# Two edits to a fused transformer-and-MoE kernel: where the last jobs' normalisation stands, and which instruction re-orders the tokens

## The chip, the cores and the metric

The kernel runs on one core of one Trainium2 chip. The time is the device time of one execution in microseconds; for the kernel before it is the median of three runs. One core has TensorE (PE; its weight loads are PEld), VectorE (DVE), ScalarE (ACT), GpSimd (POOL) and SyncE (SP), which here only issues DMAs. Each engine works through its own list in order and waits on semaphores for the others.

## What is computed

```python
x = x + 0.5 * ffn(layernorm(x))        # 16 sequences of 256 tokens, 128 features, fp32
x = x + dilated_attention(layernorm(x))
x = x + 0.5 * ffn(layernorm(x))

def ffn(x):      # 16 heads of 8, causal; 8 experts, top 2, F = 512
    h = layernorm(x + attention(x) @ w_o, g1, b1)
    w = top-2 softmax gates of h @ wg, renormalised
    y = gelu(h @ w1[e] + bb1[e]) @ w2[e] + bb2[e]      # for the two experts of a token
    return layernorm(h + sum_e w[e] * y[e], g2, b2)
```

The dilated attention takes every fourth token (DILATION_RATE 4) of a sequence, 64 at a time, and attends inside such a slice. So each sequence has two token orders in the kernel: the natural one, which the causal attention needs, and one sorted by offset, in which the rows are held for everything else.

## The kernel before

The rows are cut into 8 chunks of two sequences (512 tokens, 4 tiles of 128). Each of the two FFN layers passes over all chunks, which makes 16 jobs: jobs 0 to 7 are the first FFN, jobs 8 to 15 the second. Two jobs make a set; a set's tokens are sorted by expert, scattered to DRAM, read back in tiles of 128 rows of one expert, put through that expert's two layers, stored, and gathered again by token. The set of jobs 14 and 15 is the last, and its gathers end the program.

For one job m the pieces are: `norm`, `norm_apply` (first layer norm, VectorE), `turn` (TensorE transposes the four tiles into a bank of `ps_ring`, ScalarE copies the bank to `xn_t`), `project` and `values` (the projections, which read `xn_t`), the attention proper (`scores`, `exps`, `weigh`, `rows`), `merge` (TensorE transposes the attention's result, ScalarE copies it to `attn_feat`), `attn_out` and the middle norm, the router, the set's expert tiles (`turn_tiles`, `first`, `second`), and at the end `gather` (GpSimd), `combine`, `end_norm`, `end_norm_apply`, `end_add` (VectorE, with a power taken on GpSimd for each norm) and `store` (SyncE).

The order of pieces in each engine's list is fixed before the kernel is built: `make_orders` gives every piece a place (a half step plus a number from the table PLACES, by kind, stretch of the program and position in the set) and sorts by it. Nothing is moved at run time.

The two places that matter here:

- **The re-ordering copies.** In `turn` (TensorE L621, ScalarE L850) the transposes write tokens in the order sorted by offset, next to each other, and ScalarE's copy puts them into natural order while it writes `xn_t`. In `merge` (TensorE L729, ScalarE L884) the transposes write natural order and ScalarE's copy writes `attn_feat` sorted by offset. The copies `project` (L860) and `long_turn` (L916) are of the same size, 128x512, without re-ordering. There are 16 jobs, so 16 copies and 64 transposes at each of the two places.
- **The end of the last two jobs.** Job 14's rows are gathered with 8 indirect DMAs (L1406, two for each tile), combined (L1235, L1241), their statistics taken (L970, L974), the variance plus epsilon written (L977), and GpSimd raises it to the power -0.5 (L1344). VectorE meanwhile centres the rows and multiplies by g2 / 2 (`scale_centred`, L1201) and then adds them, scaled by the power, to the rows held in `xs` (`add_scaled`, L1212). Job 15 does the same tile by tile (`combine_last`, L1176 to L1194), since its gathers signal tile by tile, then `finish_last` (L1224) adds. SyncE stores a job's rows in four DMAs (L591); job 14's wait for `add_scaled`, job 15's in two pairs for `finish_last`. At the end all engines' queues close with a DRAIN and a barrier (L326).

Two semaphore and buffer slots are used for these norms: END for both jobs, that is, `var_eps[:, END]` and `rstd[:, END]`.

## Time and profile before

| what | value |
|---|---|
| median of three runs | 1115.26 us (1113.8 to 1119.22) |
| the profiled execution's own time | 1125.35 us |
| its span | 1123.6 us |
| TensorE busy | 969.8 us (86%) |
| TensorE weight loads busy | 788.8 us (70%) |
| VectorE busy | 687.5 us (61%) |
| ScalarE busy | 664.3 us (59%) |
| GpSimd busy | 569.8 us (51%) |
| DMA | 182.51 MB, mean 162 GB/s |

The profiled execution is a single one and is not among the three runs; its time lies 1.75 us above its span. Busy times are sums over the whole span, which has a start in which the first chunk goes through alone, a long body in which two or three jobs and the expert tiles overlap, and an end in which only tiles, then only gathers are left. A busy share says little about what an engine is worth in one of these, so the rows below are cut by stretch.

### The profile page before, as it was taken

To read this page: it belongs to the slowest core of one execution; us is meant where nothing else is said; L and a number is where in the kernel's file an instruction comes from. 1 tells how busy PE (TensorE), PEld (TensorE's weight loads), DVE (VectorE), ACT (ScalarE), POOL (GpSimd) and SP (SyncE) were. 2 spreads that over 40 slices of the span, in tenths; PEclk is the share of its full clock that TensorE was granted. 3 is DMA by queue.
4 is the path that set the end of the run, shared out by engine and by line. 5 is a ranking of instruction groups with operands and counts; after the bars stand their busy time and mean duration, and the time that the engine had idled before them with its cause. 6 is when DMAs were issued, how large, how long until landed. Compare 5 with 4: busy or idle time off the path is not lost.

```text
span 1123.6 us, 29725 instructions
## 1 busy us (share of the span) xinstructions
PE 969.8 (86%) x10913; PEld 788.8 (70%) x10913; DVE 687.5 (61%) x2458; ACT 664.3 (59%) x1494; POOL 569.8 (51%) x693
## 2 busy tenths in 40 slices
PE   3898987999899999999899998999899988947860
PEld 2666655887677877778777877788777876846860
DVE  6657784665457865798557955697567734620234
ACT  1333533777567766777657785678667767633530
POOL 2234365334565556655564555654674466550434
PEclk9978978999889999999989998999999999986985
DMA  2496043466665556556664546566575655786741
GB/s 70 103 204 165 15 118 104 128 180 170 164 173 159 156 173 132 192 170 190 161 186 146 162 166 145 166 183 195 151 197 163 191 160 161 258 257 228 265 146 47
DMA packets 120199, 182.51 MB, mean 162 GB/s; under 512 B 13144, under 2 KB 83192, under 8 KB 120056
## 3 DMA queue, kind: packets, MB, share of 16 engines
q1 hardware_dynamic: 111864, 163.83, 50.5%
q0 software_dynamic: 8192, 16.79, 5.1%
q8 instruction: 88, 1.44, 0.5%
q14 instruction: 55, 0.45, 0.2%
HBM read 145.10 MB, written 40.19 MB: 165 GB/s over the span
## 4 chain that ended last, share of the span: by engine, by line
PE 63%; DVE 13%; ACT 7%; another core or an unknown queue 6%; issue 5%; POOL 4%; DMA 1%; SPq 0%; POOLq 0%; DVEq 0%; ACTq 0%
PE ps_ring L796 12%; PE ps_ring L787 11%; PE ps_quad L657 6%; PE ps_quad L690 6%; PE ps_quad L686 5%; PE ps_ring L703 5%; PE ps_ring L718 3%; POOL picked L1406 2%; PE ps_quad L663 2%; ACT act L908 2%; PE ps_ring L630 2%; ACT probs L870 2%; DVE shift_cols L1038 2%; PE ps_ring L707 2%
## 5 line engine op out<-in xcount | busy, mean ns | idle before, releaser
L1339 POOL TENSOR_SCALAR_AFFINE_SELECT probs<-probs 128x512 f32<-128x512 f32 x256 | 171.9, 682 | 230.7 <-ACT probs L870 226.1
L870 ACT ACTIVATE probs<-ps_quad 128x768 f32<-128x768 f32 x256 | 194.1, 807 | 126.2 <-PE ps_quad L690 104.2
L1038 DVE TENSOR_REDUCE shift_cols<-ps_quad 128x2 f32<-128x512 f32 (+3 forms) x256 | 150.0, 586 | 146.8 <-PE ps_quad L671 115.0
L796 PE MATMUL ps_ring<-weights,act 128*128 128x128 f32 x1392 | 191.9, 288 | 32.3 <-ACT act L908 25.3
L908 ACT ACTIVATE act<-ps_ring,weights 128x128 f32<-128x128 f32 x696 | 190.3, 385 | 49.3 <-PE ps_ring L787 31.2
L796 PEld LDWEIGHTS ps_ring<-weights,act 128*128 128x128 f32 x1392 | 174.6, 200 | 44.6 <-ACT act L908 28.1
L787 PE MATMUL ps_ring<-tile_t,weights 128*128 128x128 f32 x1392 | 190.7, 287 | 3.6 <-issue 2.3
L787 PEld LDWEIGHTS ps_ring<-tile_t,weights 128*128 128x128 f32 x1392 | 172.7, 198 | 21.6 <-issue 18.5
L1406 POOL DMA_INDIRECT picked<-sorted_outputs,place x128 | 123.5, 965 | 76.9 <-DVEq L1169 39.0
L1388 POOL DMA_INDIRECT sorted_rows<-h_rows,place x128 | 127.9, 999 | 58.7 <-issue 32.7
L657 PE MATMUL ps_quad<-qk,q_heads 32*128 32x256 f32 (+3 forms) x1024 | 111.3, 408 | 23.2 <-ACT probs L870 15.4
L1165 DVE TENSOR_TENSOR tile_y<-ps_ring,weights 128x128 f32<-128x128 f32 x174 | 48.3, 286 | 125.3 <-PE ps_ring L796 91.8
L1344 POOL TENSOR_TENSOR rstd<-var_eps,power 128x4 f32<-128x4 f32 x56 | 58.9, 1052 | 125.4 <-DVE var_eps L977 121.4
L878 ACT ACTIVATE attn_t<-ps_ring 128x256 f32<-128x256 f32 x128 | 49.4, 389 | 120.7 <-PE ps_ring L707 80.0
L690 PE MATMUL ps_quad<-q4s,k 32*128 32x256 f32 x1024 | 113.4, 399 | 0.0
L686 PE MATMUL ps_quad<-q4s,k 32*128 32x128 f32 x1024 | 94.2, 337 | 19.4 <-DVE shift_cols L1039 15.3
L686 PEld LDWEIGHTS ps_quad<-q4s,k 32*128 32x128 f32 x1024 | 60.9, 194 | 51.3 <-DVE shift_cols L1039 25.4
L657 PEld LDWEIGHTS ps_quad<-qk,q_heads 32*128 32x128 f32 x1024 | 58.7, 194 | 50.0 <-ACT probs L870 20.2
L703 PE MATMUL ps_ring<-probs,values 128*32 128x256 f32 x1024 | 88.5, 411 | 3.6 <-issue 2.1
L1039 DVE TENSOR_REDUCE shift_cols<-ps_quad 128x2 f32<-128x64 f32 (+3 forms) x256 | 80.5, 315 | 0.0
L663 PEld LDWEIGHTS ps_quad<-qk,q_heads 32*128 32x128 f32 x1024 | 71.2, 198 | 0.7
L663 PE MATMUL ps_quad<-qk,q_heads 32*128 32x32 f32 (+3 forms) x1024 | 67.1, 260 | 0.0
(165 smaller groups left out, 1503.9 us busy)
## 6 DMA issues: line engine op xcount, KB each, us to landing
weights<-expert_weights SPq DMA_DIRECT2D x174, 578.0 KB
tile_rows<-sorted_rows SPq DMA_DIRECT2D x56, 192.0 KB
sorted_outputs<-tile_y SPq DMA_DIRECT2D x56, 192.0 KB
query_key_parts<-qk SPq DMA_DIRECT2D x32, 256.0 KB
sorted_rows<-zeros SPq DMA_DIRECT2D x3, 1472.0 KB, 12.1
k<-query_key_parts SPq DMA_DIRECT2D x64, 64.0 KB
q<-query_key_parts SPq DMA_DIRECT2D x64, 64.0 KB
xs<-in_L_attn_x SPq DMA_DIRECT2D x32, 64.0 KB, 2.3
```

Source lines behind the costliest of these rows:

```text
L657: pe.matmul(ps_quad[:, j, 0:split], q_heads[rows, n % 2, late, :, :].rearrange("p h q -> p (h q)"), qk[rows, m % 2, 1, at:at + split], sta ...
L663: pe.matmul(ps_quad[:, j, split:9 * SLOT], q_heads[rows, n % 2, soon, :, :].rearrange("p h q -> p (h q)"), qk[rows, m % 2, 1, at:at + SLOT ...
L686: pe.matmul(ps_quad[:, i, 0:P], k4[rows, par, j, at + P:at + S], q4s[rows, n % 2, j, P:S], start=True, stop=True, tile_position=(32 * i, 0))
L690: mm = pe.matmul(ps_quad[:, i, P:3 * P], k4[rows, par, j, at:at + P], q4s[rows, n % 2, j, :], start=True, stop=True, tile_position=(32 * i ...
L703: pe.matmul(to, values[:, par, 2 * b, 4 * j + i, :], probs[:, r, i, P:3 * P], start=True, stop=False, tile_position=(0, 32 * i))
L787: mm = pe.matmul(bank(use)[:, f * P:(f + 1) * P], weights_of(k)[:, f * P:(f + 1) * P], tile_t[:, n % 2, t % BATCH, :], start=True, stop=True)
L796: mm = pe.matmul(bank(use)[:, 0:D], act[:, k % ACTS, f, :], weights_of(k)[:, F + f * D:F + (f + 1) * D], start=(f == 0), stop=(f == FC - 1))
L870: sc.activation(probs[:, r % PROBS, 2 * a:2 * a + 2, :], ps_quad[:, 2 * a:2 * a + 2, 0:3 * P], ACT.Exp, scale=HD ** -0.5).then_inc(pair_fr ...
L908: ins = sc.activation(act[:, k % ACTS, f, :], bank(use)[:, f * P:(f + 1) * P], ACT.Gelu_apprx_tanh, bias=weights_of(k)[:, 2 * F + f:2 * F ...
L1038: dve.tensor_reduce(shift_cols[:, late, groups], ps_quad[:, groups, 0:split], AX.X, ALU.max)
L1339: pool.affine_select(out=both, in_=both, compare_op=ALU.is_ge, fill=0.0, base=0, pattern=[[0, 2], [0, 2], [1, P]], channel_multiplier=-1). ...
L1406: pool.indirect_dma_start(picked[:, m % 2, n, tt, :], None, sorted_y[s % DEPTH][0:set_tiles(s) * P, :], bass.IndirectOffsetOnAxis(place[:, ...
```

## The change

Two edits, independent of each other.

**The end of the last two jobs.** The table of places puts job 15's third and fourth pair of gathers ahead of job 14's power on GpSimd, and job 14's `add_scaled` behind job 15's `combine_last` on VectorE. Job 15's variance and power now use the slot MID (free by then) in place of END, so that job 14's values stay until they are used. STRETCHES writes out the function that it replaces and changes no place.

**The token order.** TensorE's transposes in `turn` and `merge` write each column to where ScalarE's copy used to put it, and the two copies become plain ones of the whole bank.

```diff
-    "gather2": (..., (22.521, 23.93)),
-    "gather3": (..., (22.899, 26.09)),
+    "gather2": (..., (22.521, 23.1)),
+    "gather3": (..., (22.899, 23.2)),
-    "end_add": (..., (24.406, 24.351)),
+    "end_add": (..., (25.3, 24.351)),
...
             def turn(m):                                   # TensorE
                 for tt in range(TT):
-                    mm = pe.transpose(bank(("turn", m))[:, tt * P:(tt + 1) * P], xn[:, m % 4, tt, :], ident[:, :])
+                    of_seq = bank(("turn", m))[:, tt // 2 * S:tt // 2 * S + S]
+                    mm = pe.transpose(of_seq.rearrange("p (n h g) -> p h g n", h=2, g=2)[:, tt % 2, :, :],
+                                      xn[:, m % 4, tt, :], ident[:, :])
...
             def merge(m):                                  # TensorE
                 for tt in range(TT):
-                    mm = pe.transpose(bank(use)[:, tt * P:(tt + 1) * P], attn[:, tt, :], ident[:, :])
+                    of_seq = bank(use)[:, tt // 2 * S:tt // 2 * S + S].rearrange("p (r n) -> p n r", r=RATE)
+                    mm = pe.transpose(of_seq[:, P // RATE * (tt % 2):P // RATE * (tt % 2) + P // RATE, :], attn[:, tt, :],
+                                      ident[:, :])
...
             def turn(m):                                   # ScalarE
-                sc.activation(xn_t[:, :].rearrange("p (q n r) -> p q r n", q=2, r=RATE),
-                              bank(("turn", m)).rearrange("p (q r n) -> p q r n", q=2, r=RATE), ACT.Copy
-                              ).then_inc(free_sem(("turn", m)), 1)
+                sc.activation(xn_t[:, :], bank(("turn", m)), ACT.Copy).then_inc(free_sem(("turn", m)), 1)
...
             def merge(m):                                  # ScalarE
-                sc.activation(attn_feat[:, :].rearrange("p (q r n) -> p q n r", q=2, r=RATE),
-                              bank(("merge", m)).rearrange("p (q n r) -> p q n r", q=2, r=RATE), ACT.Copy
-                              ).then_inc(free_sem(("merge", m)), 1)
+                sc.activation(attn_feat[:, :], bank(("merge", m)), ACT.Copy).then_inc(free_sem(("merge", m)), 1)
...
             def combine_last():                            # VectorE
-                dve.tensor_scalar(var_eps[:, END, :], moments[:, END, :, 1], EPS, None, ALU.add
-                                  ).then_inc(var_ready[END], 1)
+                dve.tensor_scalar(var_eps[:, MID, :], moments[:, END, :, 1], EPS, None, ALU.add
+                                  ).then_inc(var_ready[MID], 1)
...
             def finish_last():                             # VectorE
-                dve.wait_ge(rstd_ready[END], m + 1)
+                dve.wait_ge(rstd_ready[MID], JOBS + 1)
-                    ins = dve.scalar_tensor_tensor(out=out_rows, in0=rows[:, tt, :], scalar=rstd[:, END, tt:tt + 1],
+                    ins = dve.scalar_tensor_tensor(out=out_rows, in0=rows[:, tt, :], scalar=rstd[:, MID, tt:tt + 1],
...
             def end_norm(m):                               # GpSimd
+                if m == JOBS - 1:
+                    return powers(MID, JOBS)
                 powers(END, m)
```

On GpSimd's list the end of the program was this: twelve gathers (job 14's eight and job 15's first four), a power, four gathers, a power.

```order
L1415 TENSOR_TENSOR picked<-picked,g_half 128x512
L1406 DMA picked<-sorted_outputs,place 128x128 x12
L1344 TENSOR_TENSOR rstd<-var_eps,power 128x4
L1406 DMA picked<-sorted_outputs,place 128x128 x4
L1344 TENSOR_TENSOR rstd<-var_eps,power 128x4
L326 UNCONDITIONAL_BRANCH
```

And it is now this, with the line numbers of the changed kernel (L1409 is the gather, L1345 the power):

```order
L1418 TENSOR_TENSOR picked<-picked,g_half 128x512
L1409 DMA picked<-sorted_outputs,place 128x128 x16
L1345 TENSOR_TENSOR rstd<-var_eps,power 128x4 x2
L327 UNCONDITIONAL_BRANCH
```

The power of job 14 moved past job 15's last four gathers; nothing else on this engine did.

On VectorE's list, before: job 14's variance, centring (L1201) and adds (L1212), then job 15's first tile.

```order
L977 TENSOR_SCALAR var_eps<-moments 128x4
L1201 SCALAR_TENSOR_TENSOR picked<-picked,moments,g_half 128x128 x4
L1212 SCALAR_TENSOR_TENSOR xs<-picked,rstd,xs 128x128 x4
L1176 SCALAR_TENSOR_TENSOR picked<-picked,gates,h_rows 128x128
L1180 SCALAR_TENSOR_TENSOR picked<-picked,gates 128x128
```

Now the end of the same list: job 15's last statistics and variance (L1193), its last centring (L1195), then job 14's adds (L1213) and job 15's (L1225).

```order
L1187 BN_AGGR moments<-stats 128x2
L1193 TENSOR_SCALAR var_eps<-moments 128x4
L1195 SCALAR_TENSOR_TENSOR picked<-picked,moments,g_half 128x128
L1213 SCALAR_TENSOR_TENSOR xs<-picked,rstd,xs 128x128 x4
L1225 SCALAR_TENSOR_TENSOR xs<-picked,rstd,xs 128x128 x4
L327 UNCONDITIONAL_BRANCH
```

Job 14's four adds moved behind all of job 15's pieces but the adds. SyncE's list has the same instructions in the same order: sixteen output stores at the end, of which job 14's four stand directly ahead of job 15's four.

## Rows read from the trace of the kernel before

**Rows 1.** Busy time by stretch: start:end us, length, busy us (count) per engine, PEclk, DMA, GB/s.
```profile
200.00:400.00 200.00, 190.42 (x2250) 158.00 (x2249) 132.70 (x494) 143.80 (x320) 96.68 (x109) 0.97 0.58 164
```

**Rows 2.** Waits of TensorE, whole span: us in total, times, longest.
```profile
PE ps_ring L796 <- ACT act L908: 25.8, 14, 15.9
PE ps_quad L657 <- ACT probs L870: 15.4, 18, 3.6
```

**Rows 3.** The page, part 4: the chain that ended last, by engine.
```profile
PE 63%; DVE 13%; ACT 7%; another core or an unknown queue 6%; issue 5%; POOL 4%; DMA 1%; SPq 0%; POOLq 0%; DVEq 0%; ACTq 0%
```

**Rows 4.** Groups of ACT copies, 128x512 each: count, busy us, mean ns, idle before.
```profile
L850 ACT ACTIVATE xn_t<-ps_ring 128x512 f32<-128x512 f32 x16 | 17.8, 1112 | 0.5 <-PE ps_ring L621 0.4
L884 ACT ACTIVATE attn_feat<-ps_ring 128x512 f32<-128x512 f32 x16 | 17.4, 1089 | 11.6 <-PE ps_ring L729 5.7 <-remote 4.9 <-PE ps_ring L787 1.1
L860 ACT ACTIVATE qk<-ps_ring 128x512 f32<-128x512 f32 x16 | 9.7, 603 | 21.4 <-PE ps_ring L630 15.8 <-PE ps_ring L718 5.6
L916 ACT ACTIVATE long_xn_t<-ps_ring 128x512 f32<-128x512 f32 x8 | 4.8, 602 | 6.4 <-PE ps_ring L806 6.4
```

**Rows 5.** Chain that ended last, all four re-ordering copies on it: start, us.
```profile
14.44 1.08 ACT xn_t L850
...
166.19 1.00 ACT xn_t L850
...
178.58 1.09 ACT attn_feat L884
...
421.49 1.06 ACT attn_feat L884
```

**Rows 6.** Timeline of TensorE: start, us, line, operation, tiles, count.
```profile
606.15 0.60 PE L729 MATMUL ps_ring<-ident,attn 128*128 128x128 f32 x4
606.59 1.61 PE L787 MATMUL ps_ring<-tile_t,weights 128*128 128x128 f32 x13
```

**Rows 7.** Chain that ended last, first and last of the transposes on it.
```profile
11.97 1.10 PE ps_ring L621 x4
...
967.91 0.63 PE ps_ring L729 x4
```

**Rows 8.** Timeline of all engines in the last 20 us.
```profile
1103.71 0.94 POOL L1406 DMA_INDIRECT picked<-sorted_outputs,place  x1 [0.30 <-issue]
...
1105.01 1.13 DVE L1201 SCALAR_TENSOR_TENSOR picked<-picked,moments,g_half 128x128 f32<-128x128 f32 x4
1105.19 1.08 POOL L1344 TENSOR_TENSOR rstd<-var_eps,power 128x4 f32<-128x4 f32 x1 [0.53 <-issue]
1106.39 1.17 DVE L1212 SCALAR_TENSOR_TENSOR xs<-picked,rstd,xs 128x128 f32<-128x128 f32 x4 [0.25 <-DVE picked L1201]
1106.45 1.00 POOL L1406 DMA_INDIRECT picked<-sorted_outputs,place  x1 [0.19 <-issue]
1107.49 0.34 DVE L1176 SCALAR_TENSOR_TENSOR picked<-picked,gates,h_rows 128x128 f32<-128x128 f32 x1
...
1109.07 0.35 DVE L1176 SCALAR_TENSOR_TENSOR picked<-picked,gates,h_rows 128x128 f32<-128x128 f32 x1
...
1110.28 0.95 POOL L1406 DMA_INDIRECT picked<-sorted_outputs,place  x1 [0.30 <-issue]
...
1112.81 0.35 DVE L1176 SCALAR_TENSOR_TENSOR picked<-picked,gates,h_rows 128x128 f32<-128x128 f32 x1 [0.50 <-DMA picked<-sorted_outputs,place]
...
1114.39 1.07 POOL L1344 TENSOR_TENSOR rstd<-var_eps,power 128x4 f32<-128x4 f32 x1 [3.16 <-DVE var_eps L1192]
1115.59 1.14 DVE L1224 SCALAR_TENSOR_TENSOR xs<-picked,rstd,xs 128x128 f32<-128x128 f32 x4 [1.04 <-POOL rstd L1344]
```

**Rows 9.** SyncE's queue at the end, and the closing of the queues: durations ns min/median/max, start.
```profile
L591 SPq DMA_DIRECT2D out_rows<-xs x32: 528/606/1002, 891.0 to 1118.1; - x32
...
L326 POOLq DRAIN  x1: 9047/9047/9047, 1114.3 to 1114.3; - x1
L326 SPq COMPARE_BRANCH  x1: 41/41/41, 1120.2 to 1120.2; - x1
```

More of the change, by code:

```diff
@@ L31 @@
 SET_SIZES = (2, 2, 2, 2, 2, 2, 2, 2)
+STRETCHES = (0, 1, 2, 2, 2, 2, 3, 4)
 SETS = len(SET_SIZES)
@@ L144 @@
     "end_norm_apply": ((24.692, 25.03), (24.834, 24.887), (24.861, 25.083), (28.65, 27.9), (24.401, 23.402)),
-    "end_add": ((24.966, 25.798), (24.991, 25.316), (24.987, 25.537), (29.05, 28.521), (24.406, 24.351)),
+    "end_add": ((24.966, 25.798), (24.991, 25.316), (24.987, 25.537), (29.05, 28.521), (25.3, 24.351)),
     "store": ((), (), (26.312, 26.019), (33.935, 34.683), (29.55, 31.262)),
@@ L226, in stretch_of @@
 def stretch_of(s):
-    return {0: 0, 1: 1, SETS - 2: 3, SETS - 1: 4}.get(s, 2)
+    return STRETCHES[s]
 def make_orders():
```

4 rows, old and new, of the table PLACES are left out of this document.

## The prediction

> **What bounds the kernel now.** I read the stretches first, then what TensorE waits for, then the chain that ended last, and after that the two places that the change touches. From 200 to 400 us TensorE is busy 190.42 us of 200, ScalarE 143.80 [rows 1]; the three stretches up to 930 us look the same. So in the body of the kernel TensorE sets the pace, and ScalarE counts only where TensorE, or a transfer that it needs, is waiting for it. Those waits are few: TensorE waited 25.8 us for ScalarE's GELU, 15.9 of it in one wait near the end of the program, and 15.4 us for the exponentials [rows 2]. The chain that ended last is 63% TensorE and 7% ScalarE [rows 3]. The last 20 us are another regime: no matmul is left, and GpSimd's gathers and VectorE's short steps follow one another (part C).
>
> **Part A, ScalarE's two re-ordering copies.** The copies at L850 (16) and L884 (16) write the tokens in another order and take 1112 and 1089 ns; copies of the same 128x512 out of the same banks with no re-ordering take 603 and 602 ns [rows 4]. The changed ones are plain copies, so ScalarE is freed of 16 x (1.112 - 0.603) + 16 x (1.089 - 0.603) = 8.1 + 7.8 = 15.9 us. What is that worth? Four of the 32 copies stand on the chain that ended last, at 14.44, 166.19, 178.58 and 421.49 us [rows 5]. Behind the other 28 the chain runs over TensorE, and the copy ends before its reader's turn in TensorE's order. Four copies at 0.5 us each give **-2.0 us**. The bounds are 0 (what arrives earlier is not wanted earlier) and -15.9 (every copy counts). I take the chain's count because TensorE has next to no idle time that a faster copy could fill.
>
> **Part B, the transposes that now write scattered.** Nothing is added or removed on TensorE: 16 x 4 transposes at L621 and 16 x 4 at L729, 128 in all, of the same 128x128. What changes is where the columns land: next to each other before, now 4 words apart (turn) or 64 words apart with a step back after each four (merge). No row of the kernel before shows TensorE writing single words apart. Four transposes take 0.60 us, each 0.27, so they start (0.60 - 0.27) / 3 = 0.11 us apart; the 13 matmuls behind them, which stream as many columns, start (1.61 - 0.28) / 12 = 0.11 us apart [rows 6]. So the transposes are paced like matmuls of their width, at 0.85 ns a column. The nearest row for scattered writing is ScalarE's, into its own memory: (1112 - 603) / 512 = 1.0 ns more for each element [rows 4]. Added to TensorE's pace that is 0.13 us for each transpose and 128 x 0.13 = 16.4 us in all; if instead an address a nanosecond is the limit that holds beside the streaming, only 0.15 ns of it shows and the sum is 2.5 us. The lower end is **0**: no reason gives a gain, since the same columns stream. I take 0, since 0.85 ns a column is close to that one word a nanosecond already, and the stream and the write overlap; I keep +16.4 as the other end. The Trainium skill speaks against this part: "PSUM — Partial Sum Buffer", Specifications, says that PSUM is organised in 8-byte lines and that any access that is not contiguous slows matmuls significantly. It gives no figure; if each fp32 word then cost a line of its own, twice the time of a pair, my estimate from that page would be about double the pace, 128 x 0.11 = 14 us, against 0 in my sum.
>
> **Part C, the last 20 us.** Before, GpSimd's twelfth gather starts at 1103.71 us; then it waits for job 14's variance, takes the power at 1105.19 and starts the thirteenth gather at 1106.45, 2.74 us behind the twelfth instead of the 1.25 us between plain gathers [rows 8]. With the power behind all gathers the last four come 1.49 us earlier: the last starts at 1108.79 instead of 1110.28, and its rows, with the same landing time, are there at 1112.81 - 1.49 = 1111.32. VectorE loses the wait of 0.25 us and the four adds of 1.17 us from between the jobs, so it starts job 15's first piece behind the centring, at 1105.01 + 1.13, about 1106.2, instead of 1107.49. A piece takes 1.58 us (1107.49 to 1109.07), so it would reach the fourth at 1106.2 + 3 x 1.58 = 1110.94: it still waits, 0.4 us, for the last rows. The fourth piece thus starts 1.49 us earlier and so does the last power, 1112.9 instead of 1114.39. Job 14's power, at about 1110.0 to 1111.1, lies in front of it and is hidden by that wait. VectorE then has job 14's four adds (1.17 us plus 0.25 for the settling ahead of them) to do behind the last centred piece, 1113.1 to 1114.5, while the last power ends at 1114.0; the last four adds start at 1114.5 instead of 1115.59, 1.1 us earlier.
>
> On SyncE's queue job 14's four stores, whose rows were ready at 1106.39 + 1.17 = 1107.6 us beside the gathers [rows 8], now come free at 1114.5, right ahead of job 15's four. A store holds the queue for 0.606 us [rows 9], so the queue is done at 1114.5 + 8 x 0.606 = 1119.3, where its last store started at 1118.1 and was done at 1118.7, and the last rows land 0.6 us later than at 1120.2. Which of the two sets the end? GpSimd's DRAIN begins at 1114.3 and lasts 9.05 us, to 1123.4, while SyncE had its last store landed at 1120.2 [rows 9]: the span ends with GpSimd's DRAIN, 3.2 us behind SyncE. I take it that this DRAIN follows GpSimd's own last instruction and no store, so that it begins 1.5 us earlier: **-1.5 us**, with the later stores covered by those 3.2 us. If the DRAIN follows the stores, the term is +0.6; these are its ends.
>
> **The sum.** Against the profiled execution (1125.35 us, span 1123.6): -2.0 + 0 - 1.5 = -3.5, so 1121.85. The median of the runs shown, 1115.26, is 10.1 us lower; the same terms give 1115.26 - 3.5 = **1111.8 us**, 0.3% less. About 0.5%, or 5.6 us, is what a measurement of this kernel can tell from no change, so I forecast no change that can be told.
>
> **Rival 1, slower: the scattered write paces TensorE.** Groups of four transposes stand on the chain that ended last 16 times out of 32, from 11.97 to 967.91 us [rows 7], and in the busy stretches TensorE's queue has no slack that would hide the others. At 0.13 us each the 64 on the chain cost 8.2 us, all of them 16.4; the middle is 12.3, and 1111.8 + 12.3 = 1124.1 us. It decides from 0.07 us a transpose on (9.1 us more in all, which is 3.5 eaten up and 5.6 beyond). For it: no row shows that such a write is free, and ScalarE's is not. Against: the columns already come only every 0.85 ns. The Trainium skill, by the page and section named in part B, stands on this rival's side; nothing in the kernel before tests it for words written apart.
>
> **Rival 2, faster: ScalarE's freed time counts more widely.** ScalarE works in order, so a shorter copy also moves the exponentials or GELUs right behind it in its queue, and TensorE waits for just those [rows 2]. If half of the copies count, the term is -8.0 instead of -2.0, and 1115.26 - 8.0 - 1.5 = 1105.8 us. Against it: a TensorE that is 95% busy can give back only little.
>
> **Rival 3, no change: the end follows the stores.** Job 14's stores in front of job 15's make the end 0.6 us later, and the tail gives +0.6: 1115.26 - 2.0 + 0.6 = 1113.9 us. For it: eight stores in a row on one queue with nothing else to cover them. Against: the 3.2 us between the last landing and the end.
>
> **How the numbers follow.** My forecast has 0.38, rival 3 has 0.10; both lie within 0.5%, so "same" is 0.48. Rival 1 has 0.26, rival 2 has 0.26. The range goes from rival 2's time, 1105.5, to a little past rival 1's, 1125.0; left out are full-price transposes and more than half of the copies counting. The forecast's own range, without the rivals, is 1108.5 to 1114.5 (transposes 0 to +2.5, copies 0 to -4, tail -1.5 to +0.6).
>
> **What would show it.** Right: the copies at about 0.60 us and ScalarE's busy time down by 16 us; groups of four transposes still at about 0.60 us and what follows them starting 0.11 us after the fourth; 16 gathers in a row 1.25 us apart; job 14's adds directly behind the last centred piece; GpSimd's DRAIN from about 1.5 us earlier relative to the last tile's output, and again some 9 us long. Wrong: four transposes at 1 us or more; a gap between SyncE's last landing and the end that stays at 3.2 us when the landing moves; copies that stay at 1.1 us; or TensorE's waits for GELU and exponentials down by more than the 2 us that I count.

## The result, and the profile after

| | before | changed | ratio |
|---|---|---|---|
| 20 executions each, on one chip | 1119.15 us (1112.51 to 1131.05) | 1113.37 us (1103.01 to 1123.77) | 0.9947 [0.9923, 0.9972] |
| again, on another chip (e5 below; 23 and 12 executions) | 1129.61 us | 1127.75 us | 0.9985 [0.9957, 1.0012] |
| the profiled execution's span | 1123.6 us | 1114.8 us | |

The change takes 0.3 to 0.8% off the time by the first measurement and -0.1 to 0.4% by the second. The ratios, here and below, are those on record for fast executions, so they differ a little from the quotients of the medians beside them: in the second row 8 slow ones of the kernel before and none of the changed one are left out, and the medians of the rest are 1128.3 and 1127.75 us, a quotient of 0.9995. So the gain is small, and its size is open between nothing and some 8 us. The forecast, 3.5 us less, is a ratio of 0.9969.

The two profiled executions differ by 8.8 us, and most of that is no effect of the change. Job 14's first gather starts at 1082.39 us in the changed kernel and at 1089.85 in the kernel before. But a second profile of the kernel before, e11 below, has it at 1076.80, so the body of one and the same kernel wanders by 13 us between executions (these two were on different chips). Two single traces can therefore be compared for single instructions and for a stretch counted from a mark close to it, but not for how long the body takes. That has to come from medians.

First the page of the changed kernel, part 1, busy us, share of the span and instructions:

```profile
PE 975.2 (87%) x10913; PEld 792.0 (71%) x10913; DVE 686.5 (62%) x2458; ACT 649.9 (58%) x1494; POOL 565.9 (51%) x693
```

ScalarE's busy time fell from 664.3 to 649.9 us; the profiles with the copies as they were (the kernel before twice, and e1 below) have 663.9 to 664.4, and all with plain copies and the powers left on GpSimd 649.5 to 651.0. TensorE's 975.2 beside 969.8 before is no effect of the change: e8 and e9 below do the same TensorE work and have 959.1 and 976.0. The groups of its copies, with count, busy us, mean ns of one and the idle time before them, answer to [rows 4]:

```profile
L887 ACT ACTIVATE attn_feat<-ps_ring 128x512 f32<-128x512 f32 x16 | 9.9, 616 | 9.0 <-PE ps_ring L733 3.2 <-PE ps_ring L633 2.5 <-remote 2.2
...
L855 ACT ACTIVATE xn_t<-ps_ring 128x512 f32<-128x512 f32 x16 | 9.7, 606 | 0.4 <-PE ps_ring L623 0.4
L863 ACT ACTIVATE qk<-ps_ring 128x512 f32<-128x512 f32 x16 | 9.7, 603 | 24.5 <-PE ps_ring L633 20.9 <-PE ps_ring L721 3.4
```

The two re-ordering copies are down from 1112 and 1089 ns to 606 and 616, nearly the 603 of the plain copy: 16 x 0.506 + 16 x 0.473 = 15.7 us freed. The stretch from 200 to 400 us, with the columns of [rows 1]:

```profile
200.00:400.00 200.00, 193.38 (x2293) 159.27 (x2291) 136.57 (x504) 143.80 (x325) 98.01 (x111) 0.97 0.59 167
```

TensorE sets the pace here as before, at 193.38 us of 200. Its timeline at the place of [rows 6]:

```profile
603.82 0.60 PE L733 MATMUL ps_ring<-ident,attn 128*128 128x128 f32 x4
604.26 1.95 PE L792 MATMUL ps_ring<-tile_t,weights 128*128 128x128 f32 x16
```

Four transposes that write 64 words apart take 0.60 us, and the next line starts 0.44 us behind their start; before it was 606.59 - 606.15 = 0.44 as well. The transposes of `turn`, 4 words apart, are shown with e3 below. The waits of TensorE for GELU and for the exponentials, us in total, times and longest, beside [rows 2]:

```profile
PE ps_ring L801 <- issue: 19.6, 11, 13.5
PE ps_quad L660 <- ACT probs L873: 13.7, 18, 3.5
...
PE ps_ring L801 <- ACT act L909: 7.7, 13, 1.3
```

The long wait near the end, 15.9 us before and 13.5 now, stands here under "issue" and no longer under GELU. Put together, the second matmul's two lines and the exponentials make 41.0 us; in the kernel before they make 46.3 in one profile and 40.7 in the other. So these waits tell nothing of a change of a few us.

The timeline of all engines at the end, with the columns of [rows 8] (start, us, engine, line, operation, tiles, count, and in brackets the idle time before and what ended it):

```profile
1082.39 1.03 POOL L1409 DMA_INDIRECT picked<-sorted_outputs,place  x1 [4.57 <-DMA sorted_outputs<-tile_y]
...
1101.42 0.95 POOL L1409 DMA_INDIRECT picked<-sorted_outputs,place  x1 [0.30 <-issue]
...
1102.39 1.05 POOL L1345 TENSOR_TENSOR rstd<-var_eps,power 128x4 f32<-128x4 f32 x1
...
1103.43 0.35 DVE L1190 SCALAR_TENSOR_TENSOR picked<-picked,moments,g_half 128x128 f32<-128x128 f32 x1 [0.35 <-DVE moments L1187]
1103.96 0.35 DVE L1177 SCALAR_TENSOR_TENSOR picked<-picked,gates,h_rows 128x128 f32<-128x128 f32 x1 [0.18 <-issue]
...
1105.37 0.17 DVE L1193 TENSOR_SCALAR var_eps<-moments 128x4 f32<-128x4 f32 x1
...
1105.62 1.04 POOL L1345 TENSOR_TENSOR rstd<-var_eps,power 128x4 f32<-128x4 f32 x1 [2.18 <-DVE var_eps L1193]
1105.89 1.14 DVE L1213 SCALAR_TENSOR_TENSOR xs<-picked,rstd,xs 128x128 f32<-128x128 f32 x4
1106.94 1.14 DVE L1225 SCALAR_TENSOR_TENSOR xs<-picked,rstd,xs 128x128 f32<-128x128 f32 x4
```

All sixteen gathers follow one another, and the last starts 19.03 us behind the first; two of them take 1.07 and 1.02 us, where the others take 0.95, which makes it 0.09 later than forecast. Job 14's power (1102.39) comes behind it, and VectorE, which did not wait for that power, has job 14's four adds (L1213) at 1105.89, right ahead of job 15's (L1225). Last, the closing, beside [rows 9]: durations in ns (least, median, most) and the start.

```profile
L327 POOLq DRAIN  x1: 9008/9008/9008, 1105.6 to 1105.6; - x1
...
L327 SPq COMPARE_BRANCH  x1: 41/41/41, 1113.6 to 1113.6; - x1
```

Counted from job 14's first gather:

| us behind the first gather | before | forecast | changed |
|---|---|---|---|
| last gather starts | 20.43 | 18.94 | 19.03 |
| last power starts | 24.54 | 23.05 | 23.23 |
| job 15's adds start | 25.74 | 24.65 | 24.55 |
| SyncE's last store has landed | 30.35 | 30.95 | 31.2 |
| span ends | 33.75 | 32.25 | 32.41 |

### The profile page after: what moved, and what is told of

Read it like the earlier page. It is cut to its first block and busy times, and to the rows that moved or that the text cites. A ratio compares the mean times of both kernels' runs of the same rounds, so it can differ in the third digit from the quotient of the medians.

```text
span 1114.8 us, 29725 instructions
## 1 busy us (share of the span) xinstructions
PE 975.2 (87%) x10913; PEld 792.0 (71%) x10913; DVE 686.5 (62%) x2458; ACT 649.9 (58%) x1494; POOL 565.9 (51%) x693
## 5 line engine op out<-in xcount | busy, mean ns | idle before, releaser
L1340 POOL TENSOR_SCALAR_AFFINE_SELECT probs<-probs 128x512 f32<-128x512 f32 x256 | 169.4, 673 | 228.7 <-ACT probs L873 223.6
L801 PEld LDWEIGHTS ps_ring<-weights,act 128*128 128x128 f32 x1392 | 174.7, 200 | 40.3 <-issue 29.4
L792 PEld LDWEIGHTS ps_ring<-tile_t,weights 128*128 128x128 f32 x1392 | 174.5, 200 | 20.1 <-issue 17.4
L1409 POOL DMA_INDIRECT picked<-sorted_outputs,place x128 | 123.5, 965 | 74.1 <-DVEq L1170 35.9
L693 PE MATMUL ps_quad<-q4s,k 32*128 32x256 f32 x1024 | 119.5, 406 | 3.3 <-issue 3.1
L1345 POOL TENSOR_TENSOR rstd<-var_eps,power 128x4 f32<-128x4 f32 x56 | 58.9, 1051 | 120.9 <-DVE var_eps L978 118.2
L689 PE MATMUL ps_quad<-q4s,k 32*128 32x128 f32 x1024 | 97.8, 342 | 12.9 <-DVE shift_cols L1040 10.5
L689 PEld LDWEIGHTS ps_quad<-q4s,k 32*128 32x128 f32 x1024 | 63.6, 198 | 45.3 <-issue 19.0
L660 PEld LDWEIGHTS ps_quad<-qk,q_heads 32*128 32x128 f32 x1024 | 57.5, 193 | 49.3 <-ACT probs L873 18.6
L693 PEld LDWEIGHTS ps_quad<-q4s,k 32*128 32x128 f32 x1024 | 66.3, 204 | 6.6 <-issue 6.3
L666 PEld LDWEIGHTS ps_quad<-qk,q_heads 32*128 32x128 f32 x1024 | 69.8, 198 | 1.2 <-issue 0.7
```

The source lines that it names most:

```text
L660: pe.matmul(ps_quad[:, j, 0:split], q_heads[rows, n % 2, late, :, :].rearrange("p h q -> p (h q)"), qk[rows, m % 2, 1, at:at + split], sta ...
L689: pe.matmul(ps_quad[:, i, 0:P], k4[rows, par, j, at + P:at + S], q4s[rows, n % 2, j, P:S], start=True, stop=True, tile_position=(32 * i, 0))
L693: mm = pe.matmul(ps_quad[:, i, P:3 * P], k4[rows, par, j, at:at + P], q4s[rows, n % 2, j, :], start=True, stop=True, tile_position=(32 * i ...
L792: mm = pe.matmul(bank(use)[:, f * P:(f + 1) * P], weights_of(k)[:, f * P:(f + 1) * P], tile_t[:, n % 2, t % BATCH, :], start=True, stop=True)
L801: mm = pe.matmul(bank(use)[:, 0:D], act[:, k % ACTS, f, :], weights_of(k)[:, F + f * D:F + (f + 1) * D], start=(f == 0), stop=(f == FC - 1))
L1340: pool.affine_select(out=both, in_=both, compare_op=ALU.is_ge, fill=0.0, base=0, pattern=[[0, 2], [0, 2], [1, P]], channel_multiplier=-1). ...
```

## The experiments

Time ratios are against the kernel before on the same chip, in medians, with a 95% interval. "The end" is the time from job 14's first gather to the end of the span, read from the run's own profile. "A wait for itself" is VectorE idle until an own earlier step has finished.

### e1_end_only: the end alone

The changed kernel with transposes and copies as they were before:

```diff
-                    of_seq = bank(("turn", m))[:, tt // 2 * S:tt // 2 * S + S]
-                    mm = pe.transpose(of_seq.rearrange("p (n h g) -> p h g n", h=2, g=2)[:, tt % 2, :, :],
-                                      xn[:, m % 4, tt, :], ident[:, :])
+                    mm = pe.transpose(bank(("turn", m))[:, tt * P:(tt + 1) * P], xn[:, m % 4, tt, :], ident[:, :])
...
-                sc.activation(xn_t[:, :], bank(("turn", m)), ACT.Copy).then_inc(free_sem(("turn", m)), 1)
+                sc.activation(xn_t[:, :].rearrange("p (q n r) -> p q r n", q=2, r=RATE),
+                              bank(("turn", m)).rearrange("p (q r n) -> p q r n", q=2, r=RATE), ACT.Copy
+                              ).then_inc(free_sem(("turn", m)), 1)
```

(and the same for `merge`).

> The edit to the end of jobs 14 and 15 alone; transposes and ScalarE's copies as before. My account (the end is worth 1.3 to 1.5 us, and it can be read from the first gather of job 14 on): from the start of that gather to the end of the span 32.4 us as in the changed kernel, against 33.75 before; in the whole time 0.999 of before, which lies inside the spread. Rival (the whole gain came from the end): 0.995, and more than 2 us less from the first gather on.

Measured: 1128.01 us against 1128.88, ratio 1.0002 [0.9969, 1.0035], that is -3.5 to +4.0 us. The end took 32.43 us, 1.3 less than before. The rival's 0.995 lies outside the interval. The median can't resolve a term of 1.5 us; the trace shows it in its place. One row of it is needed below, job 15's fourth piece, whose last gather starts at 1110.76:

```profile
1113.23 0.35 DVE L1177 SCALAR_TENSOR_TENSOR picked<-picked,gates,h_rows 128x128 f32<-128x128 f32 x1 [0.69 <-DMA picked<-sorted_outputs,place]
```

### e2_order_only: the transposes and copies alone

The kernel before with the opposite edit, scattered transposes and plain copies.

> The token order alone: scattered transposes and plain copies, the end as before. If ScalarE's freed 15.6 us are worth what the chain counts, 2 us, the ratio is 0.998; if they count more widely (half of the copies), 0.993. In both cases four transposes in 0.60 to 0.66 us. From the first gather of job 14 to the end 33.75 us as before.

Measured: 1126.53 us, ratio 0.998 [0.9945, 1.0014], so -2.3 us (-6.2 to +1.6). The end took 33.47 us, as before. The groups of copies:

```profile
L886 ACT ACTIVATE attn_feat<-ps_ring 128x512 f32<-128x512 f32 x16 | 9.8, 610 | 10.8 <-PE ps_ring L732 5.9 <-remote 4.9
...
L854 ACT ACTIVATE xn_t<-ps_ring 128x512 f32<-128x512 f32 x16 | 9.7, 606 | 1.8 <-PE ps_ring L622 1.7
```

Rival 1's price for this part (8.2 to 16.4 us more, less 2) lies outside the interval, and so does half of the copies counting (-7.8).

### e3_no_reordering: nobody re-orders

The changed kernel with contiguous transposes and plain copies. It leaves out the re-ordering of the tokens, so the attention works on another order of rows; the instructions are the same in number, size and place.

```diff
-                    of_seq = bank(use)[:, tt // 2 * S:tt // 2 * S + S].rearrange("p (r n) -> p n r", r=RATE)
-                    mm = pe.transpose(of_seq[:, P // RATE * (tt % 2):P // RATE * (tt % 2) + P // RATE, :], attn[:, tt, :],
-                                      ident[:, :])
+                    mm = pe.transpose(bank(use)[:, tt * P:(tt + 1) * P], attn[:, tt, :], ident[:, :])
```

> The changed kernel with its transposes writing next to each other again, as before, and the copies left plain: nobody re-orders, so the attention sees tokens in another order and its numbers differ, while all instructions and sizes are those of the changed kernel. If scattered writing by TensorE is free, the same time as the changed kernel, ratio to before 0.995 (0.992 to 0.998) and groups of four transposes at 0.60 to 0.66 us as there. If scattered writing costs TensorE 0.03 us or more for each of 128 transposes and the copies' gain hides it, this kernel is faster than the changed one by 4 us or more, ratio 0.991 or less.

Measured: 1129.75 us, ratio 0.9998 [0.996, 1.0037]; the changed kernel had 0.9947 and 0.9985. TensorE's timeline:

```profile
606.81 0.60 PE L730 MATMUL ps_ring<-ident,attn 128*128 128x128 f32 x4
607.25 0.50 PE L788 MATMUL ps_ring<-tile_t,weights 128*128 128x128 f32 x3
```

Contiguous transposes take the same 0.60 us with the same 0.44 us to the next line. The same for `turn`, first the changed kernel, which writes 4 words apart, then e3:

```profile
531.48 0.60 PE L623 MATMUL ps_ring<-ident,xn 128*128 128x128 f32 x4
...
531.65 0.60 PE L622 MATMUL ps_ring<-ident,xn 128*128 128x128 f32 x4
```

The next line starts at 532.01 and 532.18, 0.53 us behind in both. In time e3 met neither expectation: 0.9998 is above the 0.995 that the first measurement had led to. It was not run beside the changed kernel, but on e1's and e2's chip (1.0002 and 0.998), and it is clear of the 0.991 that a hidden cost of 4 us would have given. Neither the rows nor the times show a cost of the scattered write.

### e4_copies_twice: the re-ordering copies' time doubled

The kernel before, with each of the 32 re-ordering copies done twice:

```diff
+                              ).then_inc(copied_once, 1)
+                copied[0] += 1
+                sc.wait_ge(copied_once, copied[0])
+                sc.activation(xn_t[:, :].rearrange("p (q n r) -> p q r n", q=2, r=RATE),
+                              bank(("turn", m)).rearrange("p (q r n) -> p q r n", q=2, r=RATE), ACT.Copy
                               ).then_inc(free_sem(("turn", m)), 1)
```

> The kernel before with each of ScalarE's 32 re-ordering copies done twice, the second behind the first: 32 x 1.15 = 37 us more for ScalarE in the same places. If one microsecond of a copy is worth what the chain counts (4 of 32, 0.13), 4.6 us more, ratio 1.004; if it is worth half, 18 us more, ratio 1.016; if ScalarE has only slack there, 1.000.

Measured: 1140.68 us (6 executions), ratio 1.0118 [1.0076, 1.016], so +13.3 us (8.6 to 18.1). The second copies:

```profile
L857 ACT ACTIVATE xn_t<-ps_ring 128x512 f32<-128x512 f32 x16 | 17.4, 1087 | 0.5
...
L896 ACT ACTIVATE attn_feat<-ps_ring 128x512 f32<-128x512 f32 x16 | 17.0, 1064 | 0.5
```

17.4 + 17.0 = 34.4 us more on ScalarE cost 13.3, or 0.39 us for each (0.25 to 0.52), where the chain's count says 4 of 32, or 0.13. By the medians alone it is 11.8 us, or 0.34. Either is more than the chain's share and less than half.

e4's own chain (its profile's view of what ended last) shows why. Sixteen of the 32 second copies stand on it, with 14.9 us in all, near the 13.3 measured. One of them, behind its first copy, at a place where the chain of [rows 5] has none:

```profile
40.43 1.09 ACT xn_t L852
41.55 1.08 ACT xn_t L857
```

A copy that gets longer joins the chain where it was hidden before. A copy that gets shorter can't do that: it can only take its share off where it stands on the chain, as long as everything else keeps its times. Those places are few in every chain that goes back to the start (those of most changed kernels break off in the last 10 us): 4 in the kernel before, 5 in its second profile (e11; one of the five with 0.13 us only), 5 in e2 and 3 in e9, the last two with plain copies. So 0.39 x 15.7 = 6.1 us, though just inside what e2 allows, is not a price for the change.

### e5_after_again: the changed kernel again

> The changed kernel once more, beside the other experiments of this call. Both theories: the same as in the result, ratio 0.995 (0.992 to 0.997) if that result holds on another chip; if the copies are worth the chain's 2 us and the end 1.3 us, 0.997. From the first gather of job 14 to the end of the span 32.4 us.

Measured: 1127.75 us, ratio 0.9985 [0.9957, 1.0012]. The expected 0.995 is not repeated; the 0.997 of the two terms lies inside. The end took 34.20 us, which is more than before the change. The timeline shows where it went:

```profile
1109.72 0.94 POOL L1409 DMA_INDIRECT picked<-sorted_outputs,place  x1 [0.30 <-issue]
1110.11 0.29 DVE L1185 BATCH_NORM_STATS2 stats<-picked 128x6 f32<-128x128 f32 x1 [0.85 <-DVE picked L1181]
...
1110.84 0.35 DVE L1190 SCALAR_TENSOR_TENSOR picked<-picked,moments,g_half 128x128 f32<-128x128 f32 x1 [0.22 <-issue]
...
1112.23 0.35 DVE L1181 SCALAR_TENSOR_TENSOR picked<-picked,gates 128x128 f32<-128x128 f32 x1 [0.79 <-DVE picked L1177]
1112.93 0.29 DVE L1185 BATCH_NORM_STATS2 stats<-picked 128x6 f32<-128x128 f32 x1 [0.35 <-DVE picked L1181]
1113.63 0.18 DVE L1187 BATCH_NORM_AGGREGATE moments<-stats 128x2 f32<-128x6 f32 x1 [0.41 <-DVE stats L1185]
...
1115.68 1.04 POOL L1345 TENSOR_TENSOR rstd<-var_eps,power 128x4 f32<-128x4 f32 x1 [3.95 <-DVE var_eps L1193]
```

VectorE sat idle 0.85, 0.22, 0.79, 0.35 and 0.41 us, 2.6 us in all, four times with its next step waiting for its own last one and once under "issue". In the changed kernel's first profile there is one such gap, 0.35 us at 1103.43. The 0.18 us at 1103.96, under "issue", is more likely the wait for the last rows: it ends 2.54 us behind the start of the last gather (1101.42), and in e1, where that wait is named, it is 1113.23 - 1110.76 = 2.47. In the last 20 us of the old order there is none between job 15's pieces. The 0.25 us ahead of job 14's adds, which [rows 8] put down to L1201, end 0.12 us behind the end of the power that these adds need (1105.19 + 1.08), and e11's profile names that power for it.

### e6, e7: GpSimd's powers moved to ScalarE

From the e1 and e5 profiles the end looked as if it were set by GpSimd's last power plus a fixed time. Both experiments take the powers of jobs 14 and 15 from GpSimd and let ScalarE compute them; e6 also gives job 14's four stores to ScalarE's queue, e7 leaves them on SyncE's.

```diff
+            sc.wait_ge(table_set, len(NEW_TABLE))
+            sc.activation(one_out[:, :], ones_bf[:, 0:1], ACT.Abs_reciprocal_sqrt)
+            for which, n in ((END, JOBS - 2), (MID, JOBS)):
+                sc.wait_ge(var_ready[which], n + 1)
+                sc.activation(rstd[:, which, :], var_eps[:, which, :], ACT.Abs_reciprocal_sqrt
+                              ).then_inc(rstd_ready[which], 1)
...
             def end_norm(m):
-                if m == JOBS - 1:
-                    return powers(MID, JOBS)
-                powers(END, m)
+                if m < JOBS - 2:
+                    powers(END, m)
```

> The changed kernel, with the powers of jobs 14 and 15 on ScalarE (reciprocal square root, its table loaded while it is idle) and job 14's four stores on ScalarE's queue. If GpSimd's DRAIN lasts 9 us from its own last instruction, now the last gather, it ends 20.0 + 9.0 = 29.0 us behind the first gather; SyncE's four stores are issued by 27.6 and landed by 29.3; the span ends 29.6 us behind the first gather, 2.8 less than the changed kernel, and the whole is 0.0025 lower than the changed kernel's ratio. If the DRAIN follows the stores, it starts 9 us ahead of wherever they end and lengthens with them, to 11 us or more here.

> As the last one, but all eight stores stay on SyncE's queue. DRAIN by itself: it ends 29.0 us behind the first gather, while the eight stores hold SyncE's queue to 24.6 + 8 x 0.606 = 29.5 and land at 31.2; the span ends there, 31.5 us behind the first gather, and the stores have become the bound. DRAIN behind the stores: it still ends the span, 1 to 3 us behind the last landing, 32.4 or more.

Measured: e6 1122.64 us, ratio 0.993 [0.9901, 0.9959], on the same chip as e5; its end took 29.48 us. e7, one execution: 1124.75 us, its end 31.93 us. The timeline of e6 and its closing:

```profile
1109.97 0.95 POOL L1423 DMA_INDIRECT picked<-sorted_outputs,place  x1 [0.30 <-issue]
...
1114.05 0.20 ACT L964 ACTIVATE rstd<-var_eps 128x4 f32<-128x4 f32 x1 [7.72 <-DVE var_eps L1208]
...
1115.42 1.13 DVE L1240 SCALAR_TENSOR_TENSOR xs<-picked,rstd,xs 128x128 f32<-128x128 f32 x4
1115.53 2.64 ACTq L970 DMA_DIRECT2D out_rows<-xs  x4
1116.06 2.48 SPq L592 DMA_DIRECT2D out_rows<-xs  x4
```

```profile
L327 POOLq DRAIN  x1: 20432/20432/20432, 1098.4 to 1098.4; - x1
...
L327 SPq COMPARE_BRANCH  x1: 41/41/41, 1120.0 to 1120.0; - x1
```

and of e7:

```profile
1110.26 0.95 POOL L1415 DMA_INDIRECT picked<-sorted_outputs,place  x1 [0.30 <-issue]
...
1112.45 0.35 DVE L1197 SCALAR_TENSOR_TENSOR picked<-picked,moments,g_half 128x128 f32<-128x128 f32 x1 [0.49 <-DVE moments L1194]
...
1113.85 0.29 DVE L1192 BATCH_NORM_STATS2 stats<-picked 128x6 f32<-128x128 f32 x1 [0.34 <-DVE picked L1188]
...
1116.08 5.07 SPq L592 DMA_DIRECT2D out_rows<-xs  x8
```

```profile
L327 POOLq DRAIN  x1: 20573/20573/20573, 1098.5 to 1098.5; - x1
...
L327 SPq COMPARE_BRANCH  x1: 41/41/41, 1122.6 to 1122.6; - x1
```

GpSimd's DRAIN ends 7.9 us behind the end of GpSimd's own last instruction whichever that is. After the power it is 1115.5 to 1123.4 before the change and 1106.7 to 1114.6 after it. After the last gather it is 1110.9 to 1118.8 in e6 and 1111.2 to 1119.1 in e7. It is the same 7.9 in the other ten profiles. That is not the 9 us that the expectations counted from the last gather: the DRAIN ended 27.9 us behind the first gather in e6, not 29.0. Its length in the row (9.0 us or 20.5) depends only on when it was dispatched. In e6 and e7 SyncE's COMPARE_BRANCH, the end of its wait for the stores, comes behind the DRAIN and sets the end. So here the stores have taken over. The second queue in e6 is worth about 2 us, by one profile of each: e6's end is 2.45 us shorter than e7's, of which 0.4 is that its last adds came earlier (24.50 against 24.90 us behind the first gather).

### e8, e9: each half of the end's edit

e8 is the changed kernel with the two pairs of gathers back behind job 14's power; e9 has job 14's adds back ahead of job 15's pieces.

```diff
-    "gather2": (..., (22.521, 23.1)),
+    "gather2": (..., (22.521, 23.93)),
-    "gather3": (..., (22.899, 23.2)),
+    "gather3": (..., (22.899, 26.09)),
```

```diff
-    "end_add": (..., (25.3, 24.351)),
+    "end_add": (..., (24.406, 24.351)),
```

> The changed kernel with its gathers where they were (job 14's power ahead of job 15's last four), VectorE's adds of job 14 at the end. If the gathers set when the last rows land and VectorE only follows, the last power is 24.5 us behind the first gather, as before, and the span ends 33.7 us behind it: VectorE's move gives nothing by itself. If the adds between the jobs were the bound, the last power comes at 23.3 and the end at 32.5.

> The changed kernel with VectorE's adds of job 14 where they were, ahead of job 15's first piece, and GpSimd's power of job 14 behind all gathers. VectorE then waits for a power that ends about 21.1 us behind the first gather, adds (1.2), and does job 15's four pieces (6.3) after that: last power at 28.9, end of the span 38 us behind the first gather, against 33.7 before. If VectorE were not held there, 32.4.

Measured, one execution each: the end took 33.88 us in e8 and 37.76 in e9, near the expected 33.7 and 38. The timeline of e8, and then of e9:

```profile
1101.07 0.39 DVE L1177 SCALAR_TENSOR_TENSOR picked<-picked,gates,h_rows 128x128 f32<-128x128 f32 x1 [1.06 <-DMA picked<-sorted_outputs,place]
...
1103.62 0.35 DVE L1177 SCALAR_TENSOR_TENSOR picked<-picked,gates,h_rows 128x128 f32<-128x128 f32 x1 [0.84 <-DMA picked<-sorted_outputs,place]
...
1105.19 1.07 POOL L1345 TENSOR_TENSOR rstd<-var_eps,power 128x4 f32<-128x4 f32 x1 [3.11 <-DVE var_eps L1193]
```

```profile
1100.03 1.05 POOL L1345 TENSOR_TENSOR rstd<-var_eps,power 128x4 f32<-128x4 f32 x1
1101.21 1.14 DVE L1213 SCALAR_TENSOR_TENSOR xs<-picked,rstd,xs 128x128 f32<-128x128 f32 x4 [4.98 <-POOL rstd L1345]
...
1108.57 1.04 POOL L1345 TENSOR_TENSOR rstd<-var_eps,power 128x4 f32<-128x4 f32 x1 [7.49 <-DVE var_eps L1193]
```

With VectorE's move alone the later rows (waits of 1.06 and 0.84 us for the gathers) eat what was gained. With GpSimd's alone VectorE stands 4.98 us before job 14's adds, because the power now sits behind all gathers, and everything of job 15 is behind those adds. Neither half is worth anything by itself, and the second alone would cost 4 us.

### e10, e11, e12: three more profiles of the end

The changed kernel, the kernel before and e6's kernel, once each on a third chip, beside e9.

> The changed kernel once more, for one look at its end. So far 32.4 and 34.2 us from the first gather to the end, the second with 2.6 us of VectorE waiting for its own last step. If these waits come by chance with the changed order, some of them again, and 32.4 plus their sum less about 0.5; if the one look was a freak, 32.4 and no such wait.

> The kernel before once more, for one look at its end. If VectorE's waits for its own last step belong to the changed order, none here and 33.6 us from the first gather to the end, as in the three looks at this order so far; if they can hit any order, some here too.

> Powers and job 14's stores on ScalarE once more: 29.5 us from the first gather to the end if VectorE has no such waits, up to 31.5 if it has.

Measured: the end took 32.55 us (e10), 33.50 (e11) and 29.31 (e12), in times of 1120.72, 1112.05 and 1109.2 us. VectorE waited 0.26 us for itself in e10 and not at all in e11 and e12. The first gather of e11, which shows how far the body wanders beside the 1089.85 us of the first profile:

```profile
1076.80 1.03 POOL L1406 DMA_INDIRECT picked<-sorted_outputs,place  x1 [4.34 <-DMA sorted_outputs<-tile_y]
```

The end over all profiles, in us:

| order at the end | ends | mean | VectorE's waits for itself |
|---|---|---|---|
| old (before, e2, e4, e11) | 33.75, 33.47, 33.64, 33.50 | 33.6 | none |
| new (changed, e1, e3, e5, e10) | 32.41, 32.43, 33.18, 34.20, 32.55 | 33.0 | 0.4, 0, 1.6, 2.6, 0.3 |
| new, powers alone on ScalarE (e7) | 31.93 | | 1.1 |
| new, powers and stores on ScalarE (e6, e12) | 29.48, 29.31 | 29.4 | none |

## Why the prediction was right, point by point

**The total.** 3.5 us less was forecast. Both measurements' intervals hold it (3.1 to 8.6 us less, and 4.9 less to 1.4 more), and the second also holds no change at all, so this agreement alone proves little. That the measured 1113.37 us is so near to 1111.8 is partly luck: the forecast started from the median of three executions, 1115.26, which is 3.9 us below the 1119.15 of twenty, and the drop came out 2.3 us larger than forecast, so the two misses nearly cancel. "No change that can be told" held in the second measurement; in the first the change, 0.53%, is just at the 0.5% that the forecast set and clear of no change. The forecast's own range, 1108.5 to 1114.5, doesn't follow from the terms in its bracket: they give 1115.26 - 4 - 1.5 = 1109.8 to 1115.26 + 2.5 + 0.6 = 1118.4; the measured time lies inside both. The three terms stand on different ground.

**Part A, ScalarE's copies, -2.0.** The freed time came as counted (15.7 us for 15.9). What it is worth is known only roughly from the times: e2 gives -2.3 with -6.2 to +1.6, which holds the forecast and leaves out rival 2's half of all copies. For the step "I take the chain's count" the chains speak: in no chain that goes back to the start do more than 5 of the 32 copies stand, before the change or after it, so 2.0 to 2.5 us is what shortening them can give while all else keeps its times. For copies made longer the same count is three times too small, 0.13 instead of 0.39, since e4's chain has 16. The prediction named "TensorE's waits for GELU and exponentials down by more than the 2 us" as a sign of being wrong. They are down by 46.3 - 41.0 = 5.3 in the first pair of profiles, but the kernel before has 40.7 in its second, so the sign can't be read.

**Part B, the scattered transposes, 0.** Right, and shown by the rows: 0.60 us for four and 0.44 us to what follows, contiguous (e3) or scattered 64 words apart, and 0.60 and 0.53 us for `turn`. That leaves out the small price too, whose 0.02 us for each transpose would make the 0.44 us 0.52. The pace of 0.85 ns a column holds for words 64 apart too. Rival 1 falls, and with it the page that stood on its side, the Trainium skill's "PSUM — Partial Sum Buffer", Specifications: what it says of access that is not contiguous slowing matmuls doesn't hold for these fp32 transposes, where my estimate from it was 14 us and the runs show none.

**Part C, the end, -1.5.** The mechanism was right step by step: the gathers 1.25 us apart, the last power first thing behind the last variance, the DRAIN following GpSimd's own last instruction, and the stores hidden behind it, with 1.0 us left of the 3.2 us of cover (1113.6 to 1114.6). Rival 3 falls with e6 and e7, where DRAIN and stores come apart. The size was a little too large: 1.3 us at best, 0.6 in the mean of five profiles against four. Two steps were mis-sized. The gathers were counted at 1.25 us apart throughout, and two of them take 0.07 and 0.12 us longer; the last one starts 0.09 us later than forecast and the last power 0.18 (23.23 instead of 23.05), which is most of what is missing at best. The larger one is "A piece takes 1.58 us": in the new order VectorE often waits for its own steps between the pieces, 0 to 2.6 us in all. The mean of the new order's ends, 33.0, is the best, 32.4, and about half of these waits; the rest passes while VectorE would have waited for the last rows anyway (0.69 us in e1).

What makes VectorE wait for itself stays open. It happens in five of the nine profiles in which job 14's adds stand at the end, and in none of the five with the adds in their old place; with so few, chance is not left out (were the waits blind to the order, that split would come about once in 16 times). In e7 it happens twice (1112.45 and 1113.85) with no GpSimd instruction running, since GpSimd's last had ended at 1111.21. The Trainium skill, "SBUF — State Buffer", Who interferes with whom, has VectorE's instructions with two SBUF inputs contend with GpSimd's that read SBUF. That could stand behind e5's first gap, beside the gather at 1109.72, but not behind those two of e7.

**The halves.** The forecast counted both moves of part C as one. e8 and e9, one execution each, show that it had to: alone VectorE's move is worth nothing and GpSimd's +4 us.

**A better kernel.** e6 beats both: 0.993 [0.9901, 0.9959] against the changed kernel's 0.9985 [0.9957, 1.0012] on the same chip, by the medians 5.1 us less, and an end of 29.4 us against 33.0.

## What to carry to other kernels

When a program ends in a chain over several engines, find which engine's closing ends last and count back from that engine's own last instruction; here that was GpSimd, so each microsecond off its last instruction was one off the end until the stores took over: a better order gave 0.6 us in the mean, and taking the last step off GpSimd, with the stores on two queues, 3.6 more. Moving a wait behind other work on one engine needs the matching move on the engine that reads its result, as e9 shows. And the chain of one profile prices time taken away, not time added: of the same 32 copies 4 stood on it as they were and 16 when doubled, and what an added microsecond cost was 0.39 instead of 0.13.

## What the runs showed of the hardware that was not expected

- GpSimd's DRAIN ends 7.9 us behind the end of its last instruction, in all fourteen profiles (7.91 to 7.93), be it a power or an indirect DMA and whatever SyncE's stores do.
- A power of 128x4 numbers takes 1.04 us on GpSimd and 0.20 on ScalarE as a reciprocal square root (L964 of e6), with its table loaded early.
- TensorE writes the 128 fp32 words of a transposed row 64 or 4 words apart as fast as next to each other (0.60 us for four transposes each time), while ScalarE takes 1.11 us instead of 0.60 for a 128x512 copy with steps of that kind (e1: 1111 and 1087 ns).
- Between dependent short steps VectorE sometimes waits 0.2 to 0.85 us for its own result where it usually waits none that the profile shows (e5's rows); the cause is open.
